# First cross attention of a perceiver: 32-row f32 heads in four groups of array rows, in place of bf16 triples over the full array

## The reference, cut to what matters

```python
x = x + xattn(_layernorm(x), ctx_512, ctx_512, Wq, bq, Wk, bk, Wv, bv, Wo, bo)
# inside:
qh = (q @ Wq + bq).reshape(B, LQ, HEADS, D_K).transpose(0, 2, 1, 3)    # 4, 16, 256, 16
kh = (k @ Wk + bk).reshape(B, LKV, HEADS, D_K).transpose(0, 2, 1, 3)   # 4, 16, 4096, 16
vh = (v @ Wv + bv).reshape(B, LKV, HEADS, D_K).transpose(0, 2, 1, 3)
scores = qh kh^T / sqrt(16);  out = softmax(scores) vh;  out @ Wo + bo
```

## Time and profile before

| | us |
|---|---|
| median of 3 runs | 1429.22 (1425.99 to 1431.09) |
| span of the profiled execution | 1429.1 |
| PE busy | 1375.6 (96%) |
| DVE busy | 1055.1 (74%) |
| ACT busy | 922.1 (65%) |
| POOL busy | 287.6 (20%) |

### The profile page before, as it was taken

How to read it: one execution, slowest core, us unless ns; L and a number is a source line. 1 busy time by engine, 2 the same in 40 slices (tenths; PEclk the granted TensorE clock), 3 DMA queues, 4 the chain that set the end, 5 groups by cost and what they waited for, 6 DMA issues and landing times.

```text
span 1429.1 us, 28070 instructions
## 1 busy us (share of the span) xinstructions
PE 1375.6 (96%) x11138; PEld 846.7 (59%) x11138; DVE 1055.1 (74%) x2114; ACT 922.1 (65%) x1899; POOL 287.6 (20%) x321
## 2 busy tenths in 40 slices
PE   7799999999999999999999999999999999989998
PEld 5355555555555545555554556556557999856666
DVE  4787777787777778777778888835876778767757
ACT  5366777767777767777767666672796664448731
POOL 3354222222222222122213100000003100001210
PEclk9899999999999999999999999999999999999999
DMA  6966555346554545655454743002402320347000
GB/s 184 163 145 143 119 118 111 77 102 130 116 127 92 102 84 125 128 115 113 81 97 101 184 73 61 2 1 60 119 18 65 112 67 1 91 112 155 2 1 30
DMA packets 95587, 133.19 MB, mean 93 GB/s; under 512 B 8864, under 2 KB 70944, under 8 KB 89504
## 3 DMA queue, kind: packets, MB, share of 16 engines
q1 hardware_dynamic: 95456, 131.40, 42.3%
HBM read 94.15 MB, written 37.22 MB: 92 GB/s over the span
## 4 chain that ended last, share of the span: by engine, by line
PE 79%; ACT 8%; DVE 8%; DMA 2%; issue 2%; SPq 1%; POOL 0%; DVEq 0%; ACTq 0%
PE psum L559 16%; PE psum L540 13%; PE psum L524 13%; ACT probs L783 4%; PE psum L2132 4%; PE psum L587 3%; PE psum L2106 3%; DVE peaks L685 3%; PE psum L626 3%; PE psum L1226 2%; PE psum L2851 2%; PE psum L1623 1%; PE psum L275 1%; PE psum L2861 1%; PE psum L2814 1%
## 5 line engine op out<-in xcount | busy, mean ns | idle before, releaser
L685 DVE TENSOR_REDUCE peaks<-psum 128x1 f32<-128x512 f32 x1024 | 643.3, 684 | 197.0 <-PE psum L524 196.4
L783 ACT ACTIVATE probs<-psum 128x512 f32<-128x512 f32 x1024 | 529.0, 615 | 83.3 <-PE psum L540 79.4
L524 PE MATMUL psum<-keysT,queriesT 96*128 96x512 bf16 x1024 | 390.1, 384 | 13.2 <-DMA keysT<-key_parts 7.9
L540 PE MATMUL psum<-queriesT,keysT 98*128 98x256 bf16 x2048 | 392.4, 274 | 6.1 <-ACT queriesT L846 2.4
L540 PEld LDWEIGHTS psum<-queriesT,keysT 98*128 98x128 bf16 x2048 | 176.3, 99 | 191.7 <-ACT probs L783 72.1
L559 PE MATMUL psum<-probs,values 128*17 128x256 f32 x4096 | 245.9, 380 | 0.0
L559 PEld LDWEIGHTS psum<-probs,values 128*17 128x17 f32 x4096 | 107.2, 97 | 102.6 <-issue 27.1
L524 PEld LDWEIGHTS psum<-keysT,queriesT 96*128 96x128 bf16 x1024 | 98.6, 96 | 90.9 <-issue 56.1
L918 POOL CAST key_parts<-key_f 128x512 bf16<-128x512 f32 x57 | 34.8, 611 | 518.0 <-ACT key_f L816 511.0
L816 ACT ACTIVATE key_f<-psum,bk 128x512 f32<-128x512 f32 x59 | 40.5, 687 | 120.7 <-PE psum L587 120.6
L587 PE MATMUL psum<-ctxT,wk 128*128 128x512 f32 x128 | 69.5, 625 | 2.4 <-DVE probs L728 0.9
(11 more groups left out here) (315 smaller groups left out, 1662.5 us busy)
## 6 DMA issues: line engine op xcount, KB each, us to landing
keysT<-key_parts SPq DMA_DIRECT2D x31, 768.0 KB, 7.7
key_parts<-key_parts SPq DMA_DIRECT2D x90, 256.0 KB
keysT<-key_parts SPq DMA_DIRECT2D x31, 512.0 KB, 10.1
ctx_nat<-in_ctx_dram SPq DMA_DIRECT2D x32, 256.0 KB, 3.0
keysT<-key_parts SPq DMA_DIRECT2D x31, 256.0 KB, 11.6
ctx_in<-in_ctx_dram SPq DMA_DIRECT2D x24, 256.0 KB, 5.9
ctx_turned<-ctxT SPq DMA_DIRECT2D x24, 256.0 KB, 4.4
ctx_T<-ctx_turned SPq DMA_DIRECT2D x12, 512.0 KB, 3.8
```

Of the source, the lines that this page charges most:

```text
L524: e.matmul(ps, self.queriesT[0:ROWS, u % 2, g * GH + j, t * P:(t + 1) * P], self.keysT[0:ROWS, i % RING, j, c * BANK:(c + 1) * BANK], star ...
L540: made = e.matmul(ps[:, j * S:(j + 1) * S], self.keysT[0:AUG, i % RING, j, kt * P:(kt + 1) * P], self.queriesT[0:AUG, u % 2, g * GH + j, : ...
L685: e.tensor_reduce(self.peaks[:, i % 2, pair, c:c + 1], k.ps(("max", n)), AX.X, ALU.max).then_inc(*self.peaked.up(n))
L783: e.activation(self.probs[:, t % RINGP, e2 * GH * S:(e2 + 1) * GH * S], k.ps(("scores", t, e2)), ACT.Exp).then_inc(*self.exped.up((t, e2)))
```

## The change

The bf16 parts go. Keys and queries stay f32. A head takes 17 of 32 array rows: row 0 of its block is the negated maximum in the queries (`bk_first` and a memset of ones make it 1 in the first keys), rows 1 to 16 are the head. The two heads of an even group stand at rows 0 and 32, those of an odd group at rows 64 and 96 (`rows`). So the scores of group i and the maxima of group i + 1 are in four different groups of array rows.

- **PE**: a slot is now 2 maxima matmuls (L500, 17 x 512 moving, f32), then 4 score matmuls (L513, f32) with the heads in turn; a score bank now belongs to one head (both key tiles), and both banks are taken before the first of the four. The values go every second slot (`BLOCK = 2`), 8 matmuls (L531). The shift is 4 f32 matmuls with one output row each (L591).
- **ACT**: the exponentials are by head (L724); the bias goes in as before, into `key_f` of twice the size (L751); first keys are written straight into `keysT` (L757); queries straight into `queriesT`, which holds all batches (L770).
- **POOL** splits nothing. **SP** writes f32 keys (L870, 512 KB) and reads 16 rows per head (L882, 2 x 256 KB per group, from group 4 on; `RING = 4`).
- **Prologue**: starts at slot -25. Keys of the first four groups are projected with widened weights (`wk_wide`: a head's 16 columns at 32 h + 1) into place, the queries with `wq_wide`.

The core of the diff:

```diff
-RING = 3
+RING = 4
-FIRST = -60
-RINGP = 6
+FIRST = -25
+RINGP, BLOCK = 6, 2
...
+    def rows(self, i, j, n=TALL):
+
+        first = 32 * (GH * (i % 2) + j)
+        return slice(first, first + n)
+
+    def keys(self, i, j, own):
+        return self.keysT[self.rows(i, j), i // 2 % 2, own]
+
+    def queries(self, i, j, own=slice(0, S), n=TALL):
+        b, g = divmod(i, NG)
+        return self.queriesT[self.rows(i, j, n), b, g // 2, own]
...
-            e.matmul(ps, self.queriesT[0:ROWS, u % 2, g * GH + j, t * P:(t + 1) * P],
-                     self.keysT[0:ROWS, i % RING, j, c * BANK:(c + 1) * BANK],
+            e.matmul(ps, self.queries(i, j, slice(qt * P, (qt + 1) * P)), self.keys(i, j, slice(c * BANK, (c + 1) * BANK)),
                      start=True, stop=True).then_inc(*self.max_made.up(n))
 
         for t in range(FIRST, TOTAL + 3):
-            maxima = self.maxima(t)
+            for n in self.maxima(t):
+                find_max(n, t)
             if 0 <= t < TOTAL:
                 i, p = divmod(t, SLOTS)
                 w.wait_ge(self.shiftT_kept, i)
-            for e2 in range(2):
-                if 0 <= t < TOTAL:
-                    kt, n = 2 * p + e2, (2 * t + e2) % HALVES
-                    ps = banks.use(n, w, ("scores", t, e2), (self.exped, (t, e2)))
+                ps = [banks.use((2 * t + j) % HALVES, w, ("scores", t, j), (self.exped, (t, j))) for j in range(GH)]
+                for e2 in range(2):
+                    kt = 2 * p + e2
                     for j in range(GH):
-                        made = e.matmul(ps[:, j * S:(j + 1) * S], self.keysT[0:AUG, i % RING, j, kt * P:(kt + 1) * P],
-                                        self.queriesT[0:AUG, u % 2, g * GH + j, :], start=True, stop=True)
-                    made.then_inc(*self.scored.up((t, e2)))
-                if maxima and not e2:
-                    find_max(maxima[0], t)
-            if t % 4 == 1 and 5 <= t <= TOTAL + 1:
+                        made = e.matmul(ps[j][:, e2 * S:(e2 + 1) * S], self.keys(i, j, slice(kt * P, (kt + 1) * P)),
+                                        self.queries(i, j), start=True, stop=True)
+                        if e2:
+                            made.then_inc(*self.scored.up((t, j)))
+            if t % BLOCK == 1 and BLOCK < t <= TOTAL + 1:
...
-                for e2 in range(2):
-                    w.wait_ge(self.scored, (t, e2))
-                    e.activation(self.probs[:, t % RINGP, e2 * GH * S:(e2 + 1) * GH * S], k.ps(("scores", t, e2)),
-                                 ACT.Exp).then_inc(*self.exped.up((t, e2)))
+                for j in range(GH):
+                    w.wait_ge(self.scored, (t, j))
+                    e.activation(self.probs[:, t % RINGP, j * 2 * S:(j + 1) * 2 * S], k.ps(("scores", t, j)),
+                                 ACT.Exp).then_inc(*self.exped.up((t, j)))
...
+                elif job == "first keys":
+                    quad, c = a
+                    w.wait_ge(self.bk_in, 0)
+                    w.wait_ge(self.key_made, ("first", quad, c))
+                    e.activation(self.keysT[:, quad, c * BANK:(c + 1) * BANK], k.ps(("first keys", quad, c)), ACT.Identity,
+                                 bias=self.bk_first[:, quad:quad + 1]).then_inc(*self.first_keys.up((quad, c)))
...
+                    for j in range(GH):
+                        first, h = self.rows(i, j).start, g * GH + j
+                        e.dma_start(self.keysT[first + 1:first + TALL, i // 2 % 2, :],
+                                    self.key_dram[u, h * DH:(h + 1) * DH, :]).then_inc(*self.keys_here[i % RING].up(i))
```

More of the change, by code:

```diff
@@ L398, in plan @@
             at(FIRST + 2 * c, "turn ctx", 0, c)
-        for c in range(CH):
-            fill = FIRST + 2 * c + 3 if c else FIRST + 1
-            at(fill, "fill keys", 0, c)
-            at(fill + 1, "split rest", c)
+            at(FIRST + 2 * c + 3 if c else FIRST + 1, "first keys", 0, c)
+            at(-10 + 3 * c, "first keys", 1, c)
             at(-16 + 5 * c, "fill keys", 1, c)
             if c % 2:
-                at(fill + 2, "write parts", 0, c // 2)
-                at(-13 + 5 * c, "write parts", 1, c // 2)
+                at(-13 + 5 * c, "write keys", 1, c // 2)
         at(FIRST + 3, "turn x", 0)
-        at(FIRST + 5, "make queries", 0)
-        at(FIRST + 6, "keep queries")
-        at(FIRST + 8, "split queries", 0)
-        at(FIRST + 9, "write queries", 0)
-        for piece, slot in enumerate((10, 16, 20, 21)):
-            at(FIRST + slot, "read piece", piece)
-        at(-17, "set ones")
-        at(-17, "load x")
+        at(FIRST + 5, "make queries", 0, 0)
+        at(FIRST + 10, "make queries", 0, 1)
+        at(-6, "load x")
         for b in range(1, B):
@@ L431, in plan @@
                 if c % 2:
-                    at(slot + 7, "write parts", u, c // 2)
-        for u in range(B * KD):
-            at(UNIT * u - 50 if u else FIRST + 10, "read rows", u)
+                    at(slot + 7, "write keys", u, c // 2)
         for i in range(GROUPS):
-            if i:
-                at(SLOTS * i - 31 if i >= RING else 18 * i - 48, "read keys", i)
+            if i >= RING:
+                at(SLOTS * i - 31, "read keys", i)
             at(SLOTS * i - 2, "turn shift", i)
@@ L861, in scalar @@
                     k.stream.scalar_job(e, w, *a)
-    def pool_chunks(self):
-        for t in range(FIRST, TOTAL):
-            for job, *a in self.due.get(t, ()):
-                if job == "fill keys" and not (a[0] == 0 and a[1] in self.ON_VECTOR):
-                    yield tuple(a)
-                elif job == "make queries" and a[0]:
-                    yield "q", a[0]
-    def wait_key_f(self, w, chunk):
-        n = self.turns[chunk]
-        if n >= 2:
-            w.wait_ge(self.split_pool, ("part2",) + self.chunks[n - 2])
     def gpsimd(self, e, w):
@@ L1014, in sync @@
                     k.stream.load(e, w, a[1])
-    def read_keys(self, e, i, keys, landed, key):
-        u, g = divmod(i, UNIT_GROUPS)
-        for block, run in RUNS:
-            e.dma_start(self.keysT[block * DH:(block + run) * DH, i % RING, :, keys],
-                        self.key_dram[u, g * GH:(g + 1) * GH, PARTS - run:PARTS, :, keys].rearrange(
-                            "j i d n -> (i d) j n")).then_inc(*landed.up(key))
 class Later:
```

360 lines of the change are left out of this document (123 added, 237 removed).

## The result

| | before | after |
|---|---|---|
| median | 1431.45 us (1425.99 to 1437.36, 6 runs) | 2131.56 us (2097.76 to 2157.41, 6 runs) |
| ratio | | 1.4738 [1.4644, 1.4831] |
| profiled execution | span 1429.1 us | 2148.01 us, span 2146.2 us |

The kernel became 700 us slower, where 308 were forecast: right in sign, and far above the range (1650 to 1850).

A forecast was written before the change was run, and what follows sets the result against it. The prediction took PE's instruction stream to bound the cross attention stage. 1429.1 us plus 279 for slot pairs, 24 for side jobs and 5 for the prologue gave 1737 us, range 1650 to 1850 (also given as 1650 to 1830).

The forecast's parts named there:

- the pair: Two slots without side jobs, with one block of values: 3.83 us against 2.74, +279 us over 256 pairs.
- the side jobs: Projections, transposes and gathers between slots: one more mode entry and exit at 126 stretches behind odd slots, +24 us.
- Even slot, maxima and scores together: In even slots maxima and scores start together and share the time; scores done 1.13 us after PE enters the row groups.
- The strict-order rival: Matmuls run strictly in program order, so maxima and scores add up: 4.68 us per pair, 1955 us in all; chance 0.10.
- Handovers: Delays from scores to the exponential on ACT and from it back to PE: 0.05 us each.
- Y: Zero time of the two-slot count: when PE enters the row groups behind a block of values.
- From there to the end: Odd slot's scores, mode changes and 8 value matmuls: from Y + 1.83 to Y + 3.83.
- Prologue: Work ahead of the first exponential: 73 us against 67.9, +5 us, between -25 and +15.
- Covered work: POOL's dropped split, DVE's maxima, ACT's exponentials and key reads all cost 0 while PE is slower.
- Signs: Expected in the changed profile: L513 loads waiting for exponentials, values every 3.8 us, last exponential near 1270, lower PE busy share.
- The exponential's wait is mostly hidden: Rival: side jobs and PE running ahead cover the wait for the exponential: 1489 us, up to 1650; chance 0.06.
- the other side: Rival: only streaming counts in the slots, 2.59 us per pair against 2.74, so 1391 us, faster; chance 0.03.

The follow-up runs named there:

- e1: Changed kernel with 32 rows per head in place of 17 in scores and maxima: 1793.5 us, ratio 1.2553.
- e3: Changed kernel, still 17 rows, with the values ahead of the odd slot's maxima and scores: 2302.53 us.
- e10: Changed kernel with 32 rows and the scores ahead of the maxima in every slot: 1801.97 us, ratio 1.2605.
- e11: Kernel before the change with two banks for the scores instead of three: 1503.61 us, ratio 1.0518.
- e8: Kernel before the change with only the first 17 of the stacked rows multiplied in scores and maxima: 1693.92 us.
- e9: Changed kernel with 24 rows per head in place of 17: 1794.96 us, ratio 1.2556.
- e5: Changed kernel with 32 rows and values every fourth slot instead of every second: 1834.03 us, ratio 1.2830.
- e6: Changed kernel with 32 rows and the values ahead of the odd slot's maxima and scores: 1756.34 us, ratio 1.2287.
- e7: Changed kernel with 32 rows, four banks for the scores and three for maxima and side jobs: 1824.1 us, ratio 1.2761.
- e2: Changed kernel, still 17 rows, with values every fourth slot instead of every second: 2158.22 us, ratio 1.5085.
- e4: Changed kernel, still 17 rows, with four banks for the scores and three for the rest: 2213.32 us, ratio 1.5471.

## Why the prediction was wrong, point by point

Two causes make the 700 us. The clock is worth about 338 (2131.6 less e1's 1793.5; 304 to 364 over the six runs), which was not forecast at all; the new layout and order 363 (1793.5 less 1430.2), forecast at 308. At full clock (e1) the time lies within the range, in its upper part, because the pair was sized too low and the side jobs too high, as told below.

**The step that failed** is "a granted clock below 1 in the slots, which no gap of mine (all under 1 us) should bring". It asked the wrong question: it looked for gaps, as I had seen low clock only in the prologue where PE waits. It is not the gaps (e3, e10, e11) but the rows that the matmuls use (e1, e8, e9). Every duration of the sum came from rows at full clock, and rows 7 and 8 have 32 rows in each group, where the change has 17; I treated the two as "the same shapes". At a given clock they last the same, 1.13 us for eight in both. But the clock itself did not stay: 0.74 in the slots, where the sum has 1.00 without giving a reason other than the gaps.

The Trainium skill ("TensorE: Matmul & The Clock Gate", Part 1, "What's actually happening") says that a monitor sets the gate by how busy PE has been, the default being throttled. This trace doesn't agree if busy means occupied in time: PE is busy in all 26.00 us from 442 to 468, at 0.50.

**Even slot, maxima and scores together: right.** 283.60 and 283.61, 1.15 for both where 1.13 was forecast. The strict-order rival falls a second time: the four L513 matmuls stand behind both maxima in the program and run beside them, from 283.61, while half of the maxima's instructions start at 284.13. The rule of the Trainium skill ("TensorE: Matmul & The Clock Gate", Part 3, "The mechanism") that matmuls start and end in program order does not agree with these rows.

**Handovers: too small.** I took 0.05 from scores to exponential and 0.05 back. They are 0.19 in even slots and 0.14 back (medians). So the odd slot's scores start at Y + 2.08 in the changed kernel (2.02 in e1), not 1.83.

**From there to the end: right.** 287.73 - 285.68 = 2.05, forecast 2.00. The pair is 4.13 (4.07 in e1, where it is 287.32 - 283.25), not 3.83. With e1's pair, 0.24 x 256 = 61 us.

**Side jobs: +24 was too much.** In e1 the slots take 1248.2 us; the forecast was 896.4 + 279 + 24 = 1199.4. Of the 49 us between, the pair explains 61, which leaves side jobs at +12. This is a remainder, not measured by itself.

**Prologue: +5 was right for the order** (72.6 in e1, +4.7); with 17 rows the clock adds 9.3.

**Covered work: right.** DVE, ACT, POOL (3%, "near 4%") and the key reads bound nothing; later stages 465 us for 464.

**Signs.** L513's loads do wait for L724 (153.9 us), but the rest of the signs that hang on the clock missed: last exponential at 1681 (1321 in e1) for 1270, values every 4.1 us for 3.8. PE's busy share rose to 98%, where a fall was forecast. Matmuls at half clock count as busy for longer, but that is not all of it: e1 at full clock has 97%, and the kernel before 96%.

**Slips in the working.** The range is given once as 1650 to 1830 and later as 1650 to 1850, while five steps of 0.1 us, 128 us, would make it 1609 to 1865. Half of the hidden wait gives 1613, not 1650. The prologue counts 32 transposes, the built order has 36. None of them brings 2131.6 within reach.

**Rivals.** "The exponential's wait is mostly hidden" and "the other side" fall with 4.07 per pair at full clock. What I had not seen is that the forecast stands between two floors of nearly equal height: an even slot is a loop of 2.0 to 2.1 us, an odd one 2.05 of streaming. So moving PE's work (e5, e6, e10) or the bank (e7) changes the time by -37 to +40 us. No version tried beats the kernel before.

## What to carry to other kernels

A matmul that uses few rows of the array is not only wasteful: here 17-row matmuls took the whole engine to half its clock for half of the stage, other matmuls with it. Read the granted clock of the new stage before anything else, and when a forecast takes durations from another stage, ask whether they hold at the clock that the new stage will get; padding 17 rows to 24 (zeros in the queries) took no more time per matmul and gave back 16% of the whole.
Where a result goes to another engine and back before the next matmul may write, price the round trip (1.9 to 2.1 us here, of which the exponential is 0.60) against what can stand in it; in this stage, where loop and stream are equally long, the best order gained 2% (e6) and one more bank for the scores lost 2% (e7).

## What the runs showed of the hardware

- **The clock goes with the rows in use.** 17 rows: mean 0.74 in the slots as f32 in row groups (0.63 to 0.77 in e2 to e4), 0.77 with bf16 scores and maxima over 17 rows (e8). 24 and 32 rows: 1.00 (e9, e1). 96 and 98 rows: 1.00. PE was busy in 99% of the slots' time in the changed kernel and in e8, in 97% in e2. The rows that e1 and e9 add hold zeros on one side and still count.
- **PE's waits in these slots don't lower it**: 146 us idle in 1263 at 0.99, in stops of up to 0.8 us (e10); 55 us idle in 969 at 1.00, in stops of up to 1.1 us (e11); but 4 us idle in 1793 at 0.63 (e3).
- **At half clock streaming about doubles and little else does**: eight L513 take 2.08 for 1.13, sixteen L531 1.91 for 1.06, the pair 6.82 for 4.13.
- **The exponential starts later where the maxima's matmuls end with the scores.** From the modelled end of the scores to the exponential: 0.19 us in even slots, where both maxima end in the same moment, none in the odd slot shown (286.81 for both). The Trainium skill ("TensorE: Matmul & The Clock Gate", Part 3, "The cost: per-tile semaphore tail") says that increments of tiles are served one after the other; by its formula four tiles with four increments need some 0.15 us and two with two some 0.09, an estimate. The direction agrees with these rows, the size of the difference (0.19) doesn't. In e10 the maxima end with the scores too (286.86 and 286.85) but stand behind them in the program, and the exponential starts after 0.03: so four that end together are not enough, their order counts. No run took the increments alone away, so this cause is argued, not shown.
- **Open**: where between 17 and 24 rows the clock turns; whether it is the number of rows or something else that 17 has and 24, 32, 96 and 98 have not (it is odd; no other such number was tried); why order and banks move the clock between 0.63 and 0.77 at 17 rows and not at 32; what other matmuls among them count for (the stretch at 1.00 from 280 us and the one at 0.50 from 442 us differ in their shares of the other kinds); and why the third handover, from exponential back to scores, is 0.14 us here.
